# A bottleneck block in float32: units 1 and 2 of the first 1x1 by tiles, and another order of the moments stage on ScalarE and VectorE

## What is computed

```python
def _L0_conv_ref(x, ...):
    out = relu(_bn(conv(x, w1, 1x1: 512 -> 128) + b1, g1, be1))
    out = relu(_bn(conv(out, w2, 3x3: 128 -> 128) + b2, g2, be2))
    out = _bn(conv(out, w3, 1x1: 128 -> 512) + b3, g3, be3)
    return relu(x + softplus(residual_scale)[0] * out)

def _L1_conv_ref(x, ...):
    out = conv(x, w1, 1x1) + bias1b
    out = conv(out + bias2a, w2, 3x3) + bias2b
    out = conv(out + bias3a, w3, 1x1) + bias3b
    return relu(out * rscale + rbias + x)
```

## Time and profile before

| | |
|---|---|
| median of three runs | 282.97 us (282.18, 282.97, 284.28) |
| the profiled execution | 283.54 us, of which 281.8 us are the span of its trace |
| TensorE busy | 269.6 us, 96% of the span |
| VectorE busy | 235.8 us, 84% |
| ScalarE busy | 195.9 us, 70% |
| GpSimd busy | 30.8 us, 11% |
| chain that ended last | TensorE 84%, VectorE 8%, ScalarE 4%, transfers 1% |

### The profile page before, as it was taken

One profiled execution on the slowest core, in us unless ns is written; L12 is line 12 of the kernel. 1 busy time (PEld: TensorE's weight loads), 2 busy tenths in 40 slices (PEclk: granted clock), 3 DMA queues, 4 the chain that ended last, 5 costly groups with the idle time before them and its releaser, 6 DMA issues.

```text
span 281.8 us, 3922 instructions
## 1 busy us (share of the span) xinstructions
PE 269.6 (96%) x1482; PEld 249.7 (89%) x1482; DVE 235.8 (84%) x373; ACT 195.9 (70%) x266; POOL 30.8 (11%) x32
## 2 busy tenths in 40 slices
PE   7999999999999988999999999999999999999990
PEld 3588886899999957968898999999999999999990
DVE  1497887999999568789899799797997997979592
ACT  3487763689868649659795855976958939383683
POOL 0000001000000029918000202002002000000000
PEclk9999999999999999999999999999999999999998
DMA  7999904000000010000000000040050040523187
GB/s 247 410 426 422 422 21 178 22 0 2 0 0 0 2 38 0 2 0 1 2 0 0 0 2 0 3 199 28 2 228 0 28 202 0 228 101 130 57 343 286
DMA packets 6818, 28.44 MB, mean 101 GB/s; under 512 B 912, under 2 KB 3472, under 8 KB 5904
## 3 DMA queue, kind: packets, MB, share of 16 engines
q1 hardware_dynamic: 6512, 27.79, 24.7%
q10 hardware_dynamic: 288, 0.40, 0.4%
HBM read 15.35 MB, written 12.85 MB: 100 GB/s over the span
## 4 chain that ended last, share of the span: by engine, by line
PE 84%; DVE 8%; ACT 4%; DMA 1%; issue 1%; ACTq 0%; SPq 0%; DVEq 0%
PE ps L1120 32%; PE ps L1106 20%; PE ps L1109 10%; PE ps L1087 8%; PE ps L1078 6%; PE ps L1191 4%; ACT x L607 2%; PE ps L1174 2%; PE ps L1168 2%; DMA x<-x_dram 1%; DVE vl L804 1%; DVE x L961 1%; DVE x L919 1%; ACT at L524 0%; PE ps L1220 0%
## 5 line engine op out<-in xcount | busy, mean ns | idle before, releaser
L562 ACT ACTIVATE x<-x,shift 128x784 f32<-128x784 f32 x32 | 30.1, 948 | 12.7 <-DVE x L919 12.4
L919 DVE SCALAR_TENSOR_TENSOR x<-ps,scale,x 128x784 f32<-128x784 f32 x32 | 32.6, 1029 | 1.0 <-PE ps L1109 0.8
L924 DVE TENSOR_TENSOR xl<-x,xh 128x784 fp32r<-128x784 f32 x28 | 26.8, 994 | 7.8 <-ACT xh L569 7.8
L1120 PE MATMUL ps<-vh,wu0h 128*128 128x364 f32 (+1 forms) x96 | 32.2, 336 | 0.9 <-ACT vh L468 0.7
L1120 PE MATMUL ps<-vh,wu0l 128*128 128x364 f32 (+1 forms) x96 | 32.0, 333 | 0.0
L1120 PE MATMUL ps<-vh,wu1l 128*128 128x364 f32 (+1 forms) x96 | 32.0, 333 | 0.0
L1120 PE MATMUL ps<-vh,wu1h 128*128 128x364 f32 (+1 forms) x96 | 31.9, 333 | 0.0
L961 DVE SCALAR_TENSOR_TENSOR x<-ps,scal,x 128x784 f32<-128x784 f32 x31 | 31.4, 1026 | 0.0
L1120 PE MATMUL ps<-vl,wu0h 128*128 128x364 f32 (+1 forms) x96 | 30.8, 334 | 0.0
L569 ACT ACTIVATE xh<-x 128x1568 fp32r<-128x1568 f32 x14 | 21.1, 1509 | 2.5 <-PE ps L1109 2.4
L1120 PE MATMUL ps<-vl,wu1h 128*128 128x364 f32 (+1 forms) x96 | 21.6, 333 | 0.0
(11 more groups left out here) (203 smaller groups left out, 700.6 us busy)
## 6 DMA issues: line engine op xcount, KB each, us to landing
x<-x_dram SPq DMA_DIRECT2D x15, 784.0 KB, 7.7
out_dram<-x SPq DMA_DIRECT2D x6, 1568.0 KB, 5.2
out_dram<-x SPq DMA_DIRECT2D x7, 392.0 KB, 3.7
raw<-w_dram SPq DMA_DIRECT2D x1, 1088.0 KB, 5.1
raw<-w_dram SPq DMA_DIRECT2D x1, 576.0 KB, 8.6
raw<-w_dram SPq DMA_DIRECT2D x2, 256.0 KB, 3.1
x<-x_dram ACTq DMA_DIRECT2D x2, 196.0 KB, 4.0
x<-x_dram SPq DMA_DIRECT2D x2, 196.0 KB, 4.1
```

The costliest lines, as they stand in the source:

```text
L562: nc.scalar.activation(x_quad(q, c), x_quad(q, c), ACT.Relu, bias=shift3[:, c:c + 1]).then_inc(x1_ready, 1)
L919: nc.vector.scalar_tensor_tensor(x_quad(q, c), ps[:, bank:bank + 2, 0:N], scale3[:, c:c + 1], x_quad(q, c), ALU.mult, ALU.add).then_inc(s_ ...
L924: nc.vector.tensor_tensor(pair(xl[:, c, :]), x_quad(q, c), pair(xh[:, c, :]).bitcast(F32), ALU.subtract).then_inc(xl_ready, 1)
L1120: return nc.tensor.matmul(by_row(ps[:, bank, 0:N])[:, :, a:RW - b], wu[part][:, TILE[k] + dw, :], by_row(v[:, k, :])[:, :, b:RW - a], star ...
```

## The change

Both edits are orders of work; no instruction's shape changes but those of units 1 and 2.

- SP loads units 1 and 2 as eight tiles, each with a semaphore of its own. `tile_landed(u, c)` names it.
- Unit 1 joins `TILED`: it is split by ScalarE and VectorE, tile by tile, and TensorE takes it with one raw matmul and nine split ones in place of four raw ones. Splits of units 1 and 2 wait for their tile alone.
- Unit 0 is multiplied in the order of tiles 1, 0, 3, 2.
- In the moments stage ScalarE rectifies quad 2 before its first copy, and quads 4 and 6 one and two batches later than before (3 and 6 for 2 and 4); VectorE rectifies quad 3 before its first subtraction and quad 5 one batch earlier (3 for 4).

```diff
-        TILED = (2, 3, 4, U - 1)
+        TILED = (1, 2, 3, 4, U - 1)
...
-            return x_loaded[u % XQ], 16 * (u // XQ if u % XQ == 0 else u // XQ + 1)
+            return x_loaded[u % XQ], 16 * (u // XQ if u % XQ < 3 else u // XQ + 1)
+
+        def tile_landed(u, c):
+            if u < 3:
+                return (x0_loaded, x1_loaded, x2_loaded)[u][c], 16
+            return landed(u)
...
-            for u in range(1, XQ):
-                load_x(u)
-            for c in range(CT):
-                sync.wait_ge(x0_loaded[c], 16)
-            load_x(XQ)
-            for u in range(XQ + 1, U):
-                sync.wait_ge(x_loaded[u % XQ], 16 * ((u - 1) // XQ if u % XQ == 0 else u // XQ))
+            for u in range(1, 3):
+                for c in range(CT):
+                    sync.dma_start(x[:, u, c, :], x_in[:, u, c, :]).then_inc(tile_landed(u, c)[0], 16)
+            load_x(3)
+            for u in range(XQ, U):
+                if u < XQ + 3:
+                    for c in range(CT):
+                        sync.wait_ge(*tile_landed(u - XQ, c))
+                else:
+                    sync.wait_ge(*landed(u - XQ))
                 load_x(u)
...
+            split_high(1)
             for u in range(2, U):
                 split_high(u)
...
             normalise2_first()
+            normalise2(ACT_RELU[1])
             for i in range(BATCHES):
                 turned_high(i)
-                if i == 0:
-                    normalise2(ACT_RELU[1])
-                if i == 2:
+                if i == 3:
                     normalise2(ACT_RELU[2])
-                if i == 4:
+                if i == 6:
                     normalise2(ACT_RELU[3])
                 if i == 7:
                     normalise2(ACT_RELU[4])
...
+            split_low(1)
             for u in range(2, U):
                 split_low(u)
...
             rectify2(0)
+            rectify2(1)
             for i in range(BATCHES):
                 turned_low(i)
-                if i in (1, 4):
-                    rectify2(1 + i // 4)
+                if i == 3:
+                    rectify2(2)
...
-                if u > 0:
-                    pe.wait_ge(*landed(u))
-                for c in range(CT if u < 2 else 1):
-                    if u == 0:
-                        pe.wait_ge(x0_loaded[c], 16)
-                    last = nc.tensor.matmul(ps[:, bank, 0:N], raw[:, c, :], x[:, u, c, :], start=c == 0, stop=u < 2 and c == CT - 1)
-                if u >= 2:
+                for i, c in enumerate((1, 0, 3, 2) if u == 0 else (0,)):
+                    pe.wait_ge(*tile_landed(u, c))
+                    last = nc.tensor.matmul(ps[:, bank, 0:N], raw[:, c, :], x[:, u, c, :], start=i == 0, stop=u == 0 and i == CT - 1)
+                if u > 0:
                     for c in range(1, CT):
...
             unit1(0)
-            unit1(1)
             pe.wait_ge(w1l_ready, 1)
-            for u in range(2, U):
+            for u in range(1, U):
                 unit1(u)
```

More of the change, by code:

```diff
@@ L161, in build @@
             sem(n) for n in ("par_loaded", "w0_loaded", "w0u_loaded", "w03_loaded", "w1_loaded", "w3t_loaded"))
-        x0_loaded = [sem(f"x0_loaded{c}") for c in range(CT)]
+        x0_loaded, x1_loaded, x2_loaded = ([sem(f"x{u}_loaded{c}") for c in range(CT)] for u in range(3))
         x_loaded = [sem(f"x_loaded{i}") for i in range(XQ)]
@@ L390, in split_high @@
             def split_high(u):
-                act.wait_ge(*landed(u))
+                if u >= 3:
+                    act.wait_ge(*landed(u))
                 if u >= XS + 2:
@@ L396, in split_high @@
                     for c in range(1, CT):
+                        if u < 3:
+                            act.wait_ge(*tile_landed(u, c))
                         nc.scalar.activation(xs0[u % XS][0][:, c, :], x[:, u, c, :], ACT.Copy).then_inc(xth_ready, 1)
```

## The result

The median went from 283.12 us (282.18 to 284.47, 16 runs) to 281.98 (281.58 to 282.35, 16 runs). The ratio taken within rounds is 0.9954, 95% interval 0.994 to 0.9968: 1.3 us faster, 0.9 to 1.7. The gain is clear of the noise, but smaller than 1%. The forecast was 281.0, its range 279.8 to 282.4. The single runs also came closer together: 2.3 us apart before, 0.8 after.

The account below looks back on a forecast made before the run. TensorE, busy for 96% of the span, was taken as the bound. Start 1.3 us plus moments 0.7 made 2.0, taking the 282.97 us median to 281.0; range 279.8 to 282.4 for 8 in 10.

Parts of the forecast that it names:

- The moments: Moments stage: reordered rectifications win 0.96 us in the middle, give back 0.28 near the end; -0.7 us taken.
- the start: Start of the kernel, loads and units 0 to 2: 1.3 us saved, taken as the cap between 1.42 and 1.25.
- (a): Unit 1: one raw and nine split matmuls, 2.26 us, in place of four raw ones, 2.61: -0.35 us.
- (b): Unit 0: first matmul waits for tile 1, not tile 0, and starts 0.72 us earlier at lower clock: -0.36 us.
- the cap: First 1x1: room before units 11 and 12 limits the start's gain to 1.42 us, 1.25 with slower loads.
- (c): Start: TensorE's clock rises earlier than 9.7 us once the 0.72 us stop goes; worth nothing to 2.5 us.
- Rival 1: Start: clock rises where it did; start gives 0.71 us, moments 0.7, time 281.6; chance 0.27.
- (d): Loads of units 1 and 2 as eight tiles: later units land 0.2 us later; at worst 1.7, at best nothing.
- Rival 4: Loads: tiles slow the stream, 282.5 us at 290 GB/s, 285.0 at 200; chance 0.04, 0.02 for slower than before.
- rival 5: Start: tile 1 lands no earlier than tile 0; start gives 0.35 us, all 281.9; chance 0.04.
- Rival 3: Moments stage gives nothing, since VectorE holds low part 0 behind two rectifications, 0.72 us; time 281.7; chance 0.12.
- Rival 2: Start: before's runs have a later clock rise than its trace, so 1.0 us more is gained: 280.0; chance 0.13.

## Why the prediction was right, and what it mis-sized

- **Direction and size.** A gain of 2.0 us was forecast, 1.3 measured (1.6 between the two profiled spans). The time lies in the range and within 1%, the likeliest of the three outcomes. The moments came as forecast; the start gave 0.77 and not 1.3, and two stretches that the sum leaves out gave 0.35 and took 0.24.
- **(a) Unit 1 split, -0.35, and (b) the earlier first matmul, -0.36.** The mechanisms are there: first raw matmul at 4.78 (forecast 4.64), unit 1's low tiles at 9.4 (by 9.6). Their own worth can't be read off the end of after, since what TensorE gained beyond the cap was lost. With unit 0 in the old order and all else new, the first 1x1 ended at 44.36, 0.43 ahead of before: near the 0.35 of (a) alone. The order of unit 0, which is (b) and (c) together, was then worth 0.34 of the 0.95 that the sum leaves for it. Twelve matmuls on zeros, with neither (a) nor (b), ended the first 1x1 at 43.71, ahead of after.
- **(c) The clock.** I took the earlier rise because the 0.72 us stop was the only difference. Right: in the eleven traces without a stop the rise lay between about 4 and 7.2 us, in the three with it at 9.7, 9.8 and 10.2. Rival 1 (281.6, a rise where it was) fell, though its time is nearer to the measured one than mine.
- **The cap: the term that was mis-sized.** I sized the room by units 11 and 12, 1.42 us. Unit 10 had more in before: it landed at 26.97, its low part was ready at 29.69, and TensorE wanted it at 31.68, 1.99 us later. What I took over without a reason was that, but for the 0.2 us of (d), the landings stay where they were. The late landing moved from unit 11 to the weights and unit 10, which came 1.12 us later (28.09), and the stage got 0.77. The form of the step (TensorE ends up waiting for `xl`, the rest of the clock's gain is lost) was right; the unit and 0.5 us of its size were not. The loads waited for `xl` before units 5 and 10 to 13, 2.8 us in all where up to 1.4 was forecast; the matmuls themselves only 0.6.
- **(d) The tiled loads.** The 0.2 us that I took off the cap didn't appear: unit 4 was begun at 14.06 and with whole loads at 14.02. The Trainium skill (DMA: Bandwidth & Descriptors, Bandwidth) advises transfers of 1 MiB or more; with several of 196 KB in flight, this case shows no loss against 784 KB. Rival 4 fell with that, and rival 5 with the first raw matmul at 4.78.
- **Moments, -0.7.** Measured -0.72, twice (14.42 to 13.70, and 14.42 to 13.71 with the old start). The second product at 4.72 behind the first rectification (4.7 forecast), the low part of batch 11 at 12.26 (12.3). The give-back at ScalarE and VectorE near the end came too: of the 0.96 us won in the middle 0.72 are left. Rival 3 (moments give nothing) fell.
- **Rival 2** (the runs of before pay more than their trace). Its mechanism fits the spread, its price isn't seen: in 16 runs each those of before lie 2.3 us apart and those of after 0.8. In the other comparisons before spreads over 1.1 to 2.1 us (11 to 35 runs), the kernels with an early rise over 0.5 to 0.9 (5 to 12 runs), but for the one with unit 0's order alone, 1.4. The profiled execution of before, 283.54, was already above its median. The Trainium skill (TensorE: Matmul & The Clock Gate, on the clock gate) says that the moment of the rise varies from run to run; the spread of before agrees, though only one run of each kernel has its rise on record, so that the rise makes the spread is not shown.
- **Not foreseen.** The 0.35 us between the stages, and +0.24 at the end of the kernel. The first goes with the split of unit 1: VectorE waited 0.51 to 0.53 us for `std` in before and in the three experiments without that split (moments alone, unit 0's order, longer warm-up), and 0.15 at most in after and in all those with it. What links a wait at 102 us to an edit at 8 us no run tells; it stays open. The second lies behind ScalarE's last rows, which start at 276.24 before and 274.41 after, 1.83 ahead; behind them only the last outputs go out.
- **Why unit 10 landed later.** In all 14 traces one landing behind unit 9 is 0.7 to 1.5 us late, and it is always the first or second behind the start of that packet of instructions, which takes 0.9 to 1.1 us on one transfer engine. The packet starts when TensorE has begun 87 to 99 matmul instructions. Where it starts at 26.45 and 26.93 us (before, moments alone) unit 11 is late; where it starts between 23.62 and 26.24 (all others) it is unit 10 or the weights in front of it. It isn't the weights' transfer that does it, since with that behind unit 11 unit 10 was late all the same (packet at 23.82 to 24.46). So an earlier TensorE brings its own packet forward and cuts the room that it runs into. This goes by agreement of the traces: no run moved the packet alone. Why the first landing is spared in some of them is open.

## What to carry to other kernels

Room in front of a transfer, read from the trace of before, holds only if the landings stay where they are. So ask of each unit when it landed, not only of the one that an engine waits for, and where one landing is late, ask what made it so and whether the change moves that. A stop of under a microsecond between warm-up and real work cost several microseconds of the upper clock here, and two more matmuls on zeros close it as well as a new order does. When a gain ends at a cap, look first for a finer hand-over behind the late transfer: here splitting each unit by tiles was worth more than the whole change.

## What was unexpected of the hardware

- The stop's effect on the clock: 0.72 us closed moved the upper level from 9.7 to 5.3 us with nothing else changed, while the granted-clock row of the page showed 9 (90% or more) in every slice but the last.
- GpSimd beside VectorE: three subtractions of 128x392 took VectorE 2.12 us when the first began beside a step of GpSimd, 1.52 without. A step of VectorE on 128x4 took 1.05 us in after and 0.32 before; in both it ended within 0.02 us of GpSimd's subtraction beside it (118.66 and 119.77), so what it took was how long that still ran.
- One packet of instructions of 16 KB, a microsecond on one of 16 transfer engines, goes with a landing 0.7 to 1.5 us late in all 14 traces.
- Transfers of 196 KB, several in flight, fed the units as fast as 784 KB ones (unit 4 at 14.06 and 14.02 us).
